# First stage of a four-layer attention and feed-forward kernel as one list of 128 steps, with work moved from VectorE to ScalarE, GpSimd and TensorE

## What is computed

```python
x = x + _L0_xattn_ref(_layernorm(x), ctx, ctx)
x = x + _L0_ffn_ref(_layernorm(x), router_w, router_b, expert_w, expert_b)
x = x + _L1_xattn_ref(_layernorm(x), ctx, mask)
x = x + _L1_ffn_ref(_layernorm(x), w_r, b_r, w1, b1, w2, b2)

def _L0_xattn_ref(q, k, v):      # 8 heads of 16 of the 128 ROWS
    qk = einsum('bdm,bdn->bmn', qh, kh) * scale      # 256 x 256 scores a head
    ret = einsum('bmn,bcn->bcm', softmax(qk), vh)
def _L0_ffn_ref(x, ...):
    logits = xf @ router_w + router_b                # 16 experts
    S = softmax(logits); G, idx = top_k(S.T, 128 rows each)
    y.at[idx].add(G * (xf[idx] @ expert_w + expert_b))
```

## Time and profile before

| | before |
|---|---|
| median of 3 runs | 426.61 us |
| profiled execution, its own time | 422.43 us |
| its span | 420.2 us |
| mean granted TensorE clock | 0.841 |
| busy: PE, DVE, ACT, POOL | 279.6, 317.7, 167.6, 94.8 us |

### The profile page before, as it was taken

The page is one execution under the profiler, slowest core; times in us unless marked ns, Lnnn a source line. Parts: engine busy times, 40 slices in busy tenths (PEclk is TensorE's granted clock), DMA queues, the critical chain, the costliest instruction groups (busy, mean ns, idle before and its releaser), DMA issues.

```text
span 420.2 us, 7370 instructions
## 1 busy us (share of the span) xinstructions
PE 279.6 (67%) x1872; PEld 182.5 (43%) x1872; DVE 317.7 (76%) x989; ACT 167.6 (40%) x397; POOL 94.8 (23%) x222
## 2 busy tenths in 40 slices
PE   1134777777886877877778621001559999999996
PEld 0011333353442544444334310000438988888884
DVE  5847458899989889799986748888377888787631
ACT  4110543464654536464556500000111566445631
POOL 1101323352415224111111110000133322333200
PEclk9999975789698886899989965555555999999999
DMA  2789388959294581740000380000000000000001
GB/s 88 202 189 153 98 221 187 166 150 165 71 197 79 145 126 54 146 80 1 2 1 2 100 301 0 1 0 2 1 0 0 2 25 25 25 0 25 26 27 51
DMA packets 24379, 32.90 MB, mean 78 GB/s; under 512 B 4066, under 2 KB 22434, under 8 KB 22818
## 3 DMA queue, kind: packets, MB, share of 16 engines
q1 hardware_dynamic: 23842, 32.48, 33.5%
q10 hardware_dynamic: 512, 0.13, 0.2%
HBM read 24.02 MB, written 8.39 MB: 77 GB/s over the span
## 4 chain that ended last, share of the span: by engine, by line
DVE 35%; PE 33%; issue 12%; DMA 8%; ACT 4%; POOL 3%; SPq 2%; DVEq 1%; ACTq 1%; POOLq 0%
DVE row_max L531 7%; PE t_bank L1355 5%; PE pv_bank L1273 5%; PE pv_bank L1121 4%; DMA q_stack<-q_parts_dram 4%; DVE denom_inv L549 3%; PE score_bank L1094 3%; PE scoret_bank L1107 3%; PE t_bank L1150 2%; PE score_bank L1336 2%; DMA q_parts_dram<-q_parts 2%; ACT probs L895 2%; DMA q_stack<-neg_max 2%; PE score_bank L1303 2%; DVE junk L705 1%
## 5 line engine op out<-in xcount | busy, mean ns | idle before, releaser
L895 ACT ACTIVATE probs<-scoret_bank 128x512 f32<-128x512 f32 x128 | 73.1, 596 | 52.5 <-PE scoret_bank L1107 42.3
L531 DVE TENSOR_REDUCE row_max<-score_bank 128x2 f32<-128x512 f32 x112 | 74.4, 679 | 24.3 <-PE score_bank L1094 23.1
L1107 PE MATMUL scoret_bank<-q_stack,k_stack 98*128 98x256 bf16 (+1 forms) x256 | 54.6, 301 | 28.1 <-ACT probs L895 18.7
L1094 PE MATMUL score_bank<-k_stack,q_stack 96*128 96x256 bf16 (+1 forms) x240 | 53.6, 314 | 19.1 <-DMA q_stack<-q_parts_dram 11.0
L355 POOL TENSOR_SCALAR var_eps<-mv 128x1 f32<-128x1 f32 x48 | 9.2, 192 | 189.5 <-DVE mv L567 106.9
L1107 PEld LDWEIGHTS scoret_bank<-q_stack,k_stack 98*128 98x128 bf16 (+1 forms) x256 | 24.2, 104 | 46.6 <-ACT probs L895 20.5
L1121 PE MATMUL pv_bank<-probs,values_ones 128*32 128x256 f32 x512 | 42.0, 455 | 1.0 <-ACT probs L895 1.0
L1094 PEld LDWEIGHTS score_bank<-k_stack,q_stack 96*128 96x128 bf16 (+1 forms) x240 | 21.7, 105 | 47.8 <-issue 15.3
L1273 PE MATMUL pv_bank<-q_stack,k_stack 128*128 (+1 forms) x256 | 36.0, 285 | 0.4 <-ACT q_stack L1070 0.4
L1045 ACT COPY xnt<-score_bank 128x256 f32<-128x256 f32 x16 | 6.0, 373 | 74.6 <-PE score_bank L1294 74.6
L1273 PEld LDWEIGHTS pv_bank<-q_stack,k_stack 128*128 128x128 f32 x256 | 33.9, 202 | 1.3 <-issue 0.9
(11 more groups left out here) (182 smaller groups left out, 534.5 us busy)
## 6 DMA issues: line engine op xcount, KB each, us to landing
q_stack<-q_parts_dram SPq DMA_DIRECT2D x48, 128.0 KB, 6.9
k_parts_dram<-k_parts SPq DMA_DIRECT2D x24, 128.0 KB
q_parts_dram<-q_parts SPq DMA_DIRECT2D x24, 128.0 KB
k_stack<-k_parts_dram SPq DMA_DIRECT2D x8, 384.0 KB, 4.6
ctx_stage<-in_ctx_dram SPq DMA_DIRECT2D x8, 256.0 KB, 3.2
x_stage<-in_x_dram SPq DMA_DIRECT2D x8, 256.0 KB, 3.9
k_stack<-k_parts_dram SPq DMA_DIRECT2D x8, 256.0 KB, 5.3
xs<-in_x_dram SPq DMA_DIRECT2D x8, 256.0 KB, 7.3
```

The costliest lines, as they stand in the source:

```text
L531: dve.tensor_reduce(row_max[:, i, :, h], score_bank[bank_of][:, :].rearrange("p (m n) -> p m n", m=2), AX.X, ALU.max).then_inc(s["max_done ...
L895: act.activation(probs[:, j % PROBS, :], scoret_bank[j % 2][:, :], ACT.Exp).then_inc(s["exp_done"], 1)
L1094: ins = pe.matmul(to[:, m * D:(m + 1) * D], q_stack[0:QROWS, slot, h, b_in, m * P:(m + 1) * P], k_stack[0:QROWS, slot, h, b_in, :], start= ...
L1107: ins = pe.matmul(scoret_bank[j % 2][:, k * D:(k + 1) * D], k_stack[0:SROWS, slot, h, b_in, k * P:(k + 1) * P], q_stack[0:SROWS, slot, h, ...
```

## The change

Stage A's loops go. Every engine but SP runs `for t in range(...)`, written out, and tables say at which step an item stands (`MAX_T`, `STAGE`, `MID_K`, `SCALE_Q`, `HIGH_Q`, `MID_Q`, `CTX_T`, `TAKE_VT`, all keyed by unit or batch); SP's units are written out too. The order of scores and exponentials is that of before (24 steps and 2 steps ahead). Besides:

- `gather_parts` is one VectorE instruction over 512 columns in place of two over 256; ScalarE's two masked copies stay.
- `add_x1` goes to GpSimd; so do two small products for each normalisation (`minus_shift`: -mean/root), 24 in all.
- `scale_q` and `scale_rows` become ScalarE activations (Identity, with scale and bias).
- `take_yw` becomes one ScalarE copy of 272 columns; the biases enter as a third matmul of three bf16 rows (`split_bias`, 10 small instructions on GpSimd once).
- Buffers of the last stages lie in freed slots of `k_stack`.

```diff
-LEAD = NH
+def ahead(t):
+    if t < NH:
+        return [STEPS + t]
+    if t < STEPS:
+        return [2 * t + NH, 2 * t + NH + 1]
+    return [t + STEPS + NH] if t + STEPS + NH < LAST else []
+STAGE = {3: 9, 4: 21, **{w: STEPS * (w - 3) for w in range(5, NU)}}
+MID_Q = {2: 5, 3: 15, 4: 27, **{w: STAGE[w] + 9 for w in range(5, NU)}}
...
@@ pool
             def root_q(u):
                 inverse_root(rstd_q[:, :], mv0[:, :, 1], var16[:, :], float(C), "stats_q", "var_q", "root_q", u)
+                minus_shift(shift_q[:, :], mv0[:, :, 0], rstd_q[:, :], mean_rstd[:, 0:2], "root_q", "mean_q", "shift_q", u)
...
+            def add_x1(b, u, i, first):
+                wait_apart(pool, s["div_step"], 4 * b + 4)
...
+                pool.tensor_tensor(x_new[:, i, :], gathered[:, i, 1, :], xs[:, b, :], ALU.add).then_inc(s["x1_done"], 1)
...
+            for t in range(LAST + 3 * NH):
+                for b in range(NB):
+                    if t == NH * b + 17:
+                        root_rows(b, b % 2)
+                        keep_rows(x_new, b, b % 2)
+                for w in due(STAGE, t - 1):
+                    rest_k(w)
...
+                if t == NH + 1:
+                    split_bias()
+                for b in range(NB):
+                    if t == NH * b + 14:
+                        add_x1(b, b // 2, b % 2, b < 2)
...
@@ vector
-                dve.scalar_tensor_tensor(denom[:, i, :], odd_heads, low[:, 0:1], sum_high[:, i, :],
+                dve.scalar_tensor_tensor(gathered[:, i].rearrange("p k n -> p (k n)"), pv_bank[i][:, :], high[:, 0:1],
...
@@ scalar
+            def take_yw(b):
+                act.wait_ge(s["yw_ready"], b + 1)
+                act.copy(y_ext[:, b, :], t1_bank[:, 0:D + NE]).then_inc(s["yw_done"], 1)
...
+            def scale_rows(b, i, first):
+                if not first:
+                    act.wait_ge(s["xn_t"], b - 1)
+                act.wait_ge(s["shift_x"], b + 1)
+                act.activation(xn[:, i, :], x_new[:, i, :], ACT.Identity, bias=shift_x[:, i:i + 1],
+                               scale=rstd[:, i:i + 1]).then_inc(s["xn_ready"], 1)
...
@@ tensor
             def yw(b, i):
...
+                ins = pe.matmul(t1_bank[:, 0:D + NE], ones_bf[0:3, 0:P], bias_parts[:, :], start=False, stop=True)
```

510 lines of the change are left out of this document (183 added, 327 removed).

## The result

The changed kernel takes 488.24 us (median of 4 runs, 486.14 to 489.80). The kernel before, in the same set, took 425.75 (median of 4, 420.42 to 427.80). The ratio is 1.151, with a 95% interval from 1.139 to 1.164: 15% slower, where 410 us and 4% faster were forecast. The profiled execution took 489.8 us with a span of 488.0; that of before had a span of 420.2. The difference to explain is 67.8 us. In later sets a few executions were slowed as a whole (670.8 us once for the kernel before); the ratios leave them out, the medians do not.

The account below looks back on a forecast made before the run. VectorE was taken to bound stage A from step 16 on, except its last stretch. Terms +3 - 16.7 - 2.8 - 1.2 + 1.3 = -16.4 us took 422.43 to 406.0, ratio 0.961, or 410 us by the median; range 396 to 422.

Parts of the forecast that it names:

- VectorE's sum: Stage A, unit 3: removed and joined VectorE work takes its busy time from 23.69 to 19.1 us.
- rival C: Stage A: late q stacks become the bound, or multiply L556 waits for GpSimd; 422 us by the median; chance together 0.16.
- ScalarE's pause before `mid_k`: Units with preparation: ScalarE's 3.43 us wait for GpSimd's `k_rest` gets covered by earlier issue; some 1.5 us gained per unit.
- Beneath 21 us this stays hidden, if its waits are: ScalarE in stage A: 2.4 us more work per unit on 14.12 of 27.6 stays hidden.
- the chain from the variance to the shift: GpSimd's work before ScalarE's `scale_rows`: 1.9 us per batch, 2.5 at the upper price; exponentials queue behind the wait.
- Rival D: ScalarE's uncovered waits per batch after step 24 become the bound, slower: 438 us by the profiled execution, 443 by median; chance 0.11.
- upper level (2.4 GHz): TensorE's clock in units with preparation: about 17.8 us busy at full clock; at 0.81 it would be 22, over VectorE.
- Theory 3 of experiment 4: That run's theory, not the prediction's: TensorE's lower clock is the bound; under 470 us only with clock above 0.80.
- -16.7: Stage A, steps 24 to 79, 3.5 units at 21.5 us: 75.3 us in place of 92.0.
- +3: Step 24 comes 3 us later, as `mid_q` of unit 3 and its stacks are later; from 0 to +8.
- -2.8: Stage A, steps 80 to 103, 1.5 units at 19.5 us: 29.2 us in place of 32.0.
- 2.4 us a unit: Idle time beside VectorE's 19.1 us in a unit with preparation, left of 3.9 us; gives 21.5 us per unit.

Follow-up runs that it names:

- experiment 4: Changed kernel with `yw` one step later, its copy `take_yw` two later, and `send_neg_max` five steps after the maxima's transpose instead of three: 426.2 us.
- experiment 5: Changed kernel, order kept, with scaling of x's rows and q, addition of x and copy of the expert products back on VectorE: 490.6 us.
- experiment 2: Changed kernel with only ScalarE's `send_neg_max` moved, to five steps after the maxima's transpose instead of three: 439.4 us.
- experiment 6: Kernel before with the maxima's chain late: transpose one step later, `neg_low` behind the multiply and the send two steps later: 437.1 us against 421.3.
- the mended kernel with the early load: Changed kernel with `yw`, its copy and the sends later, and the stage load ahead of q's part writes: 417.71 us over ten runs, ratio 0.992.
- experiment 8: On the changed kernel with `yw`, `take_yw` and sends later (426.2 us), next unit's x and ctx load before q's part writes: 419.8 us, first run.
- experiment 10: On experiment 4, row scaling back on VectorE: 421.7 us. On experiment 8, `neg_low`, first sends, q earlier: 423.4; plus row scaling back: 421.0; all moves undone: 428.8.

## Why the prediction was wrong

**What was right.** VectorE's sum: 19.1 us was forecast for unit 3, and 64.28 / 3.5 = 18.4 came on the mean of such units. (The forecast took off the overlap of 9 rows of VectorE; 12 go in each unit, 166 less 124 in 3.5 units, so its 19.1 should have been 19.3.) GpSimd: 3.6 us more per unit forecast, (39.38 - 27.48) / 3.5 = 3.4 measured. The prices of unknown operations: the gather 0.73 forecast, 0.743 measured; the addition on GpSimd 0.6 and 0.722; the small products 0.2 and 0.189. VectorE's addition had a median of 0.416 us, so GpSimd takes 1.7 times as long; the Trainium skill ("GPSIMD Engine Reference", section Elementwise — side-by-side cycle accounting) says about twice. The slow multiply of rival C did not come: L605 took 424 to 437 ns in all 16 batches. ScalarE's pause before `mid_k` went: 2.4 us in three places for GpSimd's `k_rest`, none over 0.8, in place of 10.7. The later stages kept their length.

**What was too low.** ScalarE: 2.4 us more per unit forecast, (58.57 - 47.88) / 3.5 = 3.1 measured; its scaling of 256 columns takes 0.600, the exponential of 512 takes 0.597, and the forecast's 0.4 stood on no row. TensorE: the bias matmul was put at 0.1 to 0.2 us and has a median of 0.344. Neither is a cause of the 67 us: both stay in experiment 4, which has 426.2.

**The step that failed** is "Beneath 21 us this stays hidden, if its waits are". The condition was named and its chance set at one in ten, since ScalarE is busy for half of the time only. That is no argument: an engine that runs in order holds the exponentials behind every wait, however idle it is. I had priced only the chain from the variance to the shift, 2.5 us at most, and that one cost least (13.7 us over 11 batches at L904). What the runs showed in its place are two other waits: ScalarE's send behind VectorE's `neg_low` (-49 us when it alone is moved), and ScalarE and VectorE behind TensorE's block of `values` and `yw` (-20). I did not compare, for each wait of ScalarE, the step of the waiting instruction with the step of what it waits for on the other engine. The list showed both places: `neg_low` behind the multiply in the order rows of VectorE, and `yw` in the step of `values`. `neg_low` and its send the change left as they were; the copy behind `yw` it moved to ScalarE, but experiment 5, with the copy back on VectorE, is as slow. My cost part by part went through what the change adds and moves between engines, and of what it shifts by a step through `k_rest` and `mid_q` only.

**Rival D** had the right mechanism, ScalarE's waits per batch, with the wrong place and size: 2.5 us per batch, 438 us by the profiled execution and 443 by the median. Measured were 3.3 us (52.5 / 16) before L891 and 3.3 (42.9 / 13) behind the send. What such a wait costs is no fixed multiple of its length: in experiment 2 the waits behind the send fell by 30 us and the time by 49, in experiment 6 they grew by 51 and the time by 16.

**The clock.** I had put TensorE at its upper level (2.4 GHz) once the pause in unit 3 was gone. There are more pauses now. After the ones in the timeline above matmuls run at the lower level (1.2 GHz): `values` takes 1.94 us at 232.71, behind a pause of 2.8 us, and 1.07 at 240.51. Over steps 24 to 79 the granted clock was 0.76 (0.85 before), and in the last stretch 0.56 against 0.89. It falls with the waits and rises when they are taken away (0.83, 0.87). How much of the 67 us is the clock's own part was not measured, since no run changed the clock without changing the waits. Theory 3 of experiment 4 stays open in that sense.

**Where the predicted gain is.** The windows of the mended kernel with the early load, its profiled execution with a span of 414.4 us, cut at the same steps:

```profile
77.10:92.90 15.80, 10.04 (x74) 5.19 (x73) 10.73 (x22) 7.59 (x17) 6.23 (x15) 0.72 0.65 120
92.90:171.30 78.40, 64.26 (x527) 34.33 (x525) 62.63 (x118) 57.76 (x124) 38.04 (x82) 0.94 0.63 133
171.30:206.40 35.10, 28.28 (x219) 15.53 (x219) 27.32 (x50) 19.05 (x43) 7.99 (x24) 0.85 0.33 71
```

Against the kernel before, cut at exponentials too, steps 24 to 79 take 78.4 us in place of 91.2: -12.8, where -16.7 was forecast, with TensorE at a clock of 0.94. Steps 16 to 23 take 15.8 in place of 11.9, +3.9; the forecast said +3 (its reason, the late stacks of unit 3, is only a part: the maxima's transfer among them waits too). Steps 80 to 103 take 35.1 in place of 32.0, +3.1, where -2.8 was forecast. There the stacks of the last unit are late, as rival C had it: TensorE waits for them at step 88, 3.6 us in the first run of this kernel. The three together are the -5.8 us between the spans (414.4 and 420.2), so of the rest nothing is gained. Even in the mended order VectorE is busy for 62.6 of 78.4 us, 17.9 of 22.4 a unit, where the forecast had 19.1 of 21.5: its arithmetic on VectorE was nearly right, and what it took for the time beside it, 2.4 us a unit, was too little in this order as well.

## What to carry to other kernels

When an order is rewritten, go through every wait and compare the place of the waiting instruction with the place of its releaser on the other engine, counting how many steps each engine runs ahead; do it for the instructions that merely shift by a step before those that change engines. The busy share of an engine that feeds others in a ring does not tell how much it may wait: ScalarE, busy for 39% of the span, lost the time here. Nor does the sum of its waits tell what they cost. The longest wait in a profile is often where a delay arrives: move the waiting instruction alone once, and see whether the wait vanishes or only changes its line.

## What the runs showed of the hardware

Issuing two transfers from ScalarE's queue keeps it from its next exponential for 1.3 us in the batch shown above (246.01 to 247.34); L881 has a median of 0.628 us for one.

A small transfer sent into the middle of a large one lands late. The maxima of batch 3 were issued at 84.6 us, between the stacks' nine transfers, and TensorE's wait for them ended at 91.9 (experiment 8; 3.9 us of such a wait in experiment 4, at the same place). From 77 to 240 us of that run TensorE waited for the maxima nowhere else. With the first sends earlier the wait was gone in two of the three runs of experiment 10; in the third, with all moves undone, one of 3.5 us was left.

A wait of ScalarE and the time that it costs differ both ways when TensorE stands in the ring: 30 us less of waits behind the send gave back 49 in the kernel after, with the granted clock of the span going from 0.77 to 0.83; 51 us more of them cost 16 in the kernel before, with the clock at 0.83 in place of 0.84.
